# Sixteen row maxima and their scores over ten slots instead of eight, the negation and its transposition after them

## The chip, the core and the metric

The kernel runs on one core of one Trainium2 chip. Its engines are TensorE (PE; its weight loads are listed as PEld), VectorE (DVE), ScalarE (ACT), GpSimd (POOL) and SyncE (SP, which issues most DMAs). Each works through its own instructions in order and waits for the others by semaphores. The metric is the device time of one execution in microseconds (us); lower is better.

## What is computed

One transformer layer on x of shape (4, 2048, 512) in float32. After a layer norm, xn feeds two branches whose results are added to x: attention with keys and values compressed 4 to 1, followed by a Fourier transform, and a feed-forward part with a shared expert and 64 routed experts. The change touches the attention only. Its part of the reference, cut:

```python
qkv = x @ Wqkv
q, k, v = jnp.split(qkv, 3, axis=-1)
k = _compress(k, conv_w, conv_b)          # 2048 positions -> 512
v = _compress(v, conv_w, conv_b)
k = jnp.concatenate([null_k, k], axis=1)  # one key and value more
v = jnp.concatenate([null_v, v], axis=1)
dots = jnp.einsum('bhid,bhjd->bhij', q, k) * d ** (-0.5)
mask = q_idx[:, None] < k_idx[None, :]
dots = jnp.where(mask[None, None], mask_value, dots)
attn = jax.nn.softmax(dots, axis=-1)      # subtracts each row's maximum
out = jnp.einsum('bhij,bhjd->bhid', attn, v)
```

and beside it, in the same stage, the shared expert `jax.nn.silu(xf @ sh_gate_w) * (xf @ sh_up_w) @ sh_down_w` on all 8192 tokens.

## The kernel before

The program runs stage A (layer norm, projections, routing), stage B (`stage_b`, lines 610 to 1443: attention, shared expert, the routed tokens' table), stage E (routed experts) and stage C (output projection and transform). The stages follow one another; the change lies in stage B alone.

**Units.** Attention is cut into 64 units (`NU`): 16 items, one for each batch element and group of four heads, by 4 chunks of 512 queries (`NCH`, `QC`). The chunk's place in its item is n = u % 4. Chunk n needs n + 1 blocks of 128 keys, so its work grows with n.

**Why there are maxima.** A unit's scores are computed twice. First with queries on the partitions: `scores(u, i)` (L1292) for i = 0 to 15, that is four tiles of 128 queries by four heads, writes one bank of `ps_s`; `row_max(u, i)` (L1058) on VectorE reduces it to a column of `mx`. The width is 32 * (4 * n + i // 4 + 1) columns, so it grows with i and with n, up to 512. Then `negate(u)` (L1072) writes -max, split in two parts, into `nm`; `turn_max(u)` (L1316) transposes `nm` on TensorE with four transposes into a `ps_s` bank; and `max_rows(u)` (L961) on ScalarE copies eight rows of it into `q`, as additional rows. With them the second pass, `scores_t(u, kt, h)` (L1323), keys on the partitions, gives scores less their row's maximum, which `exponent` (L967) turns into weights. `scores_null` and `null_exponent` do the same for the additional key.

**The banks.** There are two banks of `ps_s`, used in turn by the sixteen scores and the transposition (`ring_before` L757, `s_bank` L766): 17 uses in a unit. A score waits until the maximum before the last has been read; number 0 waits for the last but one use, number 1 for `max_rows` of the unit before.

**The order.** The order of work is written out by hand, for each engine on its own: a loop over the units, in it a loop over 12 slots k (`SLOTS`), in which each engine takes what is listed for k. In unit u the engines work on the second pass of unit u and on the first pass of unit u + 1. TensorE's slot (L1418 to L1443) begins with six matmuls of 512 columns of the shared expert (`gate_up` in even units and in slots 0 to 3 of odd ones, `down` else). Then come two scores of the next unit (k < 8), up to two `scores_t` (slots 0 to 9 at most), `values` (attention times values, packed matmuls; own chunk in slot 6, others in 7, 9, 11), `denominators` and, in slot 10, `turn_max(u + 1)` and `scores_null(u)`. The first `scores_t` of a unit waits for `mt_emptied`, that is for `max_rows`.

VectorE's slot (L1233 to L1284) holds `up_out`, `gate_out`, `down_out` and `split_h` of the shared expert, `normalise` (slot 1) and `invert` (slots 2 to 5) of the unit before, two `row_max` of the next unit (k < 8), `negate` in slot 8, `add_past` (slots 6, 8, 10 for n = 1, 2, 3 of them) and one step of `group` (L1134), which builds the table of the routed tokens: 16 groups of 36 steps, three units each, so from unit 1 to unit 48. GpSimd masks the diagonal block, multiplies the result (`finish`) and from unit 4 to 51 scatters the table's pairs by indirect DMAs (`scatter`, L931).

TensorE needs from VectorE, in its slots, `gate_out` before slots 4, 8 and the next 0 (semaphore `g_emptied`), `up_out` two slots after it, `down_out(0)` before slot 8 in odd units (`y_emptied`), and the maxima as told above. SyncE loads q two units ahead (`load_q`, L786), once the null scores of the unit before are computed.

Of the kernel before, what the change touches and what calls it, by code (L numbers as in the profile page):

```python
# [599 lines left out]
NU = ITEMS * NCH  # L600
# [9 lines left out]
def stage_b(nc, t):  # L610
    ctx = ExitStack()
    with ctx:
# [153 lines left out]
        def s_bank(u, i):  # L766
            return ps_s[(17 * u + i) % 2]

        def steps(u):

            return u // 2, u % 2 == 0
# [4 lines left out]
        def chunk(part, i):  # L776

            i %= 6
            if i < HJ:
                return part[0][:, i, :, :, :].rearrange("p a k n -> p (a k n)")  # L780
            i -= HJ
            return part[1][:, 2 * i:2 * i + 2, :].rearrange("p j c -> p (j c)")
# [167 lines left out]
        @block.scalar  # L950
        def _(act):
            def split_w(i):
                act.wait_ge(raw_in[i % 2], 32 * (i // 2 + 1))
                j = i % 6
                if i >= 6 and j < HJ:
                    act.wait_ge(u_filled, HJ * (NSTEP - 1) + j + 1)
                elif i >= 6:
                    act.wait_ge(y_filled, TPB * NSTEP)
                act.copy(chunk((wgu_hi, wd_hi), i), raw[i % 2][:, :]).then_inc(w_hi_ready, 1)

            def max_rows(u):  # L961

                act.wait_ge(mt_filled, u + 1)
                act.copy(q[u % 3][3 * DH:KM, :, :], s_bank(u, 16)[3 * DH:KM, None, :].broadcast_to([2 * HPC, HPC, QC]))\
                    .then_inc(mt_emptied, 1)

            def exponent(u, kt, h):  # L967
                i, n = t_index(u, kt, h), u % NCH
                act.wait_ge(t_filled, i + 1)
                if kt == n:  # L970
                    dst = p_diag
                    if u and h == 0:
                        act.wait_ge(pv_done, pv_index(u - 1, (u - 1) % NCH) + 1)
                        if (u - 1) % NCH:
                            act.wait_ge(dve_summed, past_index(u - 1, 0) + 1)
                        else:
                            act.wait_ge(d_filled, u)
                else:
                    c = past_index(u, kt)
                    dst = p_past[c % 2]  # L980
                    if c >= 2 and h == 0:
                        act.wait_ge(pv_done, pv_of_past[c - 2] + 1)
                        act.wait_ge(dve_summed, c - 1)
                act.activation(dst[:, h, :], ps_t[i % 2][:, :], ACT.Exp, scale=SCALE).then_inc(t_emptied, 1)

            pv_of_past = [pv_index(u, kt) for u in range(NU) for kt in range(u % NCH)]

            def null_exponent(u):
                i = t_null(u)
                act.wait_ge(t_filled, i + 1)  # L990
                if u:
                    act.wait_ge(od_emptied, u)
                act.activation(p_null[:, :], ps_t[i % 2][:, :], ACT.Exp, scale=SCALE).then_inc(t_emptied, 1)

            def half_tanh(s, j):
                n = s * HJ + j
                act.wait_ge(g_filled, n + 1)
                if n:
                    act.wait_ge(h_ready, n)
                act.activation(gated[:, :], ps_f[0][:, :], ACT.Tanh, scale=0.5).then_inc(tanh_ready, 1)  # L1000

            def split_h(s, j):
                act.wait_ge(h_ready, s * HJ + j + 1)
                if s:
                    act.wait_ge(y_filled, TPB * s)
                act.copy(hT_hi[:, j, :], hT[:, :]).then_inc(h_hi_ready, 1)

            split_w(0)
            max_rows(0)
            for u in range(NU):  # L1010
                s, gate = steps(u)
                n = u % NCH
                for k in range(SLOTS):
                    if gate and k % 4 == 2:
                        half_tanh(s, k // 4)
                    if gate and k in (5, 9):
                        split_h(s, k // 4 - 1)
                        if s == NSTEP - 1:
                            split_w(6 + k // 4 - 1)
                    if not gate and k == 1:  # L1020
                        split_h(s, 2)
                        if s == NSTEP - 1:
                            split_w(6 + 2)
                    if not gate and k == 2:
                        half_tanh(s, 3)
                    if not gate and k == 4:
                        split_h(s, 3)
                        if s == NSTEP - 1:
                            split_w(6 + 3)
                    if gate and s == NSTEP and k in (3, 4):  # L1030
                        split_w(10 + k - 3)
                    for kt, h in t_slots(n, k):
                        exponent(u, kt, h)
                    if u == 0 and k in (1, 3, 7, 9, 10):
                        split_w((1, 3, 7, 9, 10).index(k) + 1)
                    if k == 11:
                        if u + 1 < NU:
                            max_rows(u + 1)
                        null_exponent(u)

        @block.vector
        def _(dve):
# [189 lines left out]

            for u in range(NU):  # L1233
                s, gate = steps(u)
                for k in range(SLOTS):
                    if gate:
                        if k == 0 and s:
                            down_out(s - 1, 3)
                        if k in (4, 8):
                            up_out(s, k // 4 - 1)  # L1240
                        if k in (6, 10):
                            split_h(s, (k - 6) // 4)
                            if s == NSTEP - 1:
                                split_w(6 + (k - 6) // 4)
                        if k % 4 == 3:
                            gate_out(s, k // 4)
                        if s == NSTEP and k in (5, 7):
                            split_w(10 + (k - 5) // 2)
                    else:
                        if k == 0:  # L1250
                            up_out(s, 2)
                        if k == 2:
                            split_h(s, 2)
                            if s == NSTEP - 1:
                                split_w(8)
                        if k == 3:
                            gate_out(s, 3)
                        if k == 4:
                            up_out(s, 3)
                        if k == 5:  # L1260
                            split_h(s, 3)
                            if s == NSTEP - 1:
                                split_w(9)
                        if k in (7, 8, 10):
                            down_out(s, k // 2 - 3 if k > 7 else 0)
                    if k == 1 and u:
                        normalise(u - 1)
                    if 2 <= k < QTC + 2 and u:
                        invert(u - 1, k - 2)
                    if u + 1 < NU:  # L1270
                        if k < 8:
                            row_max(u + 1, 2 * k)
                            row_max(u + 1, 2 * k + 1)
                        if k == 8:
                            negate(u + 1)
                    if u == 0 and k in (1, 3, 7, 9, 10):
                        split_w((1, 3, 7, 9, 10).index(k) + 1)
                    if k == 9 and u % NCH == 0 and 2 <= u // NCH + 1 < ITEMS:
                        place_null(u // NCH + 1)
                    if k in (6, 8, 10) and (k - 6) // 2 < u % NCH:  # L1280
                        add_past(u, (k - 6) // 2)
                    g, part = (u - 1) // GU_UNITS, (u - 1) % GU_UNITS
                    if 0 <= g < NG:
                        group(g, part * SLOTS + k)  # L1284
# [6 lines left out]
        def _(pe):  # L1291
# [126 lines left out]
            for u in range(NU):  # L1418
                s, gate = steps(u)
                n = u % NCH  # L1420
                for k in range(SLOTS):
# [3 lines left out]
                        gate_up(s, HJ - 1, k // 2, k % 2)  # L1425
                    else:
                        down(s, *DOWNS[k - 4])
                    if u + 1 < NU and k < 8:
                        scores(u + 1, 2 * k)
                        scores(u + 1, 2 * k + 1)  # L1430
                    for kt, h in t_slots(n, k):
                        scores_t(u, kt, h)
                    for kt in pv_slots(n, k):
# [3 lines left out]
                    if k == 0 and u and (u - 1) % NCH:  # L1437
                        denominators(u - 1)
                    if k == 10:
                        if u + 1 < NU:  # L1440
                            turn_max(u + 1)
                        scores_null(u)
            denominators(NU - 1)  # L1443


# [855 lines left out]
```

## Time and profile before

| | us |
|---|---|
| median of 3 runs | 5639.76 |
| lowest and highest | 5633.38, 5650.49 |
| the profiled execution | 5632.38 |
| its span | 5630.6 |

In the profile the table of stretches gives for a stretch of the span the busy time and the number of instructions of each engine, the granted share of TensorE's clock and the DMA engines' share. A wait is idle time of an engine, put down to the instruction whose semaphore ended it; "issue" is time for which nothing is shown, "remote" a signal whose sender isn't shown. The recorded start of a matmul is when it is taken up, its end is modelled. A `DVE_READ_ACCUMULATOR2_ANT` row is the second half of a `row_max` and overlaps what follows, so start to start counts for VectorE.

### The profile page before, as it was taken

The page shows a single profiled execution, that of the slowest core. Times are in us where ns is not written, and L with a number is a line of the kernel's source. Part 1 is how long each engine was busy: PE and PEld are TensorE (multiplying, and loading weights), DVE is VectorE, ACT ScalarE, POOL GpSimd, SP SyncE. Part 2 cuts the span into 40 slices and gives each one's busy share as a digit, 9 for nine tenths or more (in the row PEclk, how much of TensorE's full clock was granted, in tenths as well). Part 3 has the DMA queues.
Part 4 walks back from the last instruction along what each step waited for, and adds up shares of the span by engine and source line. Part 5 has one row for each costly group of instructions (what it writes and reads, how often), then busy time and mean ns, then how long its engine had stood idle before and what let it go on. Part 6 is the DMA issues. An engine that isn't in the chain of part 4 may idle for free. (4 is left out here: it accounts for less than half of the span.)

```text
span 5630.6 us, 101187 instructions
## 1 busy us (share of the span) xinstructions
PE 5462.3 (97%) x33072; PEld 4555.4 (81%) x33072; DVE 3849.7 (68%) x7136; ACT 2578.8 (46%) x3737; POOL 2996.2 (53%) x2620
## 2 busy tenths in 40 slices
PE   8999979999999999999899999999999999999999
PEld 7888866666666666776899999999999999999886
DVE  5444438887778877776666666666666666666656
ACT  3222223333333333333566666666666666666510
POOL 2222202555555555411677777777777777777514
PEclk9999989999999999999999999999999999999999
DMA  6555454434444344432667667677788667676648
GB/s 222 179 179 179 172 161 121 120 110 135 117 129 128 111 130 122 128 113 90 142 116 155 127 130 178 133 156 156 166 206 195 134 118 171 134 155 112 153 173 286
DMA packets 478101, 836.09 MB, mean 148 GB/s; under 512 B 54273, under 2 KB 159490, under 8 KB 475251
## 3 DMA queue, kind: packets, MB, share of 16 engines
q1 hardware_dynamic: 337011, 541.90, 30.3%
q0 software_dynamic: 140928, 292.13, 28.9%
q8 instruction: 90, 1.47, 0.1%
q14 instruction: 72, 0.59, 0.0%
HBM read 501.55 MB, written 332.30 MB: 148 GB/s over the span
## 5 line engine op out<-in xcount | busy, mean ns | idle before, releaser
L1649 POOL DMA_INDIRECT mid_base<-e_rows,e_ox x556 | 1179.0, 2120 | 371.1 <-POOL e_ox L1644 255.7
L1758 DVE TENSOR_TENSOR e_wgu_lo<-e_wgu,e_wgu_hi 128x2048 fp32r<-128x2048 f32 x278 | 637.3, 2292 | 812.5 <-ACT e_wgu_hi L1681 728.8
L1637 POOL DMA_INDIRECT e_xg<-mid_xn,e_ix x556 | 623.2, 1121 | 338.8 <-POOL e_ix L1634 228.0
L1694 ACT CAST e_xT_hi<-e_ps_t 128x512 fp32r<-128x512 f32 x556 | 298.9, 590 | 951.8 <-PE e_ps_t L1824 951.8
L935 POOL DMA_INDIRECT mid_ids<-b_pairs,b_cell x512 | 608.7, 1189 | 148.9 <-issue 147.5
L1837 PE MATMUL e_ps_g<-e_xT_hi,e_wgu_hi 128*128 128x256 f32 x2224 | 652.6, 293 | 1.7 <-DVE e_gated L1775 1.7
L1837 PE MATMUL e_ps_g<-e_xT_lo,e_wgu_hi 128*128 128x256 f32 x2224 | 629.6, 283 | 0.0
L1837 PE MATMUL e_ps_g<-e_xT_hi,e_wgu_lo 128*128 128x256 f32 x2224 | 629.5, 283 | 0.0
L1837 PE MATMUL e_ps_u<-e_xT_hi,e_wgu_lo 128*128 128x256 f32 x2224 | 629.4, 283 | 0.0
L1837 PE MATMUL e_ps_u<-e_xT_hi,e_wgu_hi 128*128 128x256 f32 x2224 | 629.4, 283 | 0.0
L1837 PE MATMUL e_ps_u<-e_xT_lo,e_wgu_hi 128*128 128x256 f32 x2224 | 629.4, 283 | 0.0
L1681 ACT CAST e_wgu_hi<-e_wgu 128x2048 fp32r<-128x2048 f32 x278 | 531.6, 1912 | 28.8 <-DMA e_wgu<-in_up_w 28.8
L1069 DVE CUSTOM_DVE_ANT_0 b_ps_s<-b_ps_s,b_mask 128x34 f32<-128x34 f32 (+14 forms) x960 | 387.3, 440 | 138.3 <-PE b_ps_s L1311 109.1
L1849 PE MATMUL e_ps_y<-e_wd_hi,e_hT_hi 128*128 128x512 f32 x1112 | 436.2, 392 | 0.0
L1849 PE MATMUL e_ps_y<-e_wd_lo,e_hT_hi 128*128 128x512 f32 x1112 | 436.0, 392 | 0.0
L1849 PE MATMUL e_ps_y<-e_wd_hi,e_hT_lo 128*128 128x512 f32 x1112 | 433.6, 390 | 0.0
L1387 PE MATMUL b_ps_f<-b_xT_hi,b_wgu_hi 128*128 128x512 f32 x1024 | 423.0, 413 | 8.5 <-DVE b_gated L1113 8.4
L1837 PEld LDWEIGHTS e_ps_g<-e_xT_hi,e_wgu_hi 128*128 128x128 f32 x2224 | 426.2, 192 | 2.1 <-issue 2.1
L1837 PEld LDWEIGHTS e_ps_g<-e_xT_lo,e_wgu_hi 128*128 128x128 f32 x2224 | 427.6, 192 | 0.0
L1837 PEld LDWEIGHTS e_ps_u<-e_xT_hi,e_wgu_hi 128*128 128x128 f32 x2224 | 427.0, 192 | 0.0
L1837 PEld LDWEIGHTS e_ps_u<-e_xT_lo,e_wgu_hi 128*128 128x128 f32 x2224 | 427.0, 192 | 0.0
L1837 PEld LDWEIGHTS e_ps_u<-e_xT_hi,e_wgu_lo 128*128 128x128 f32 x2224 | 427.0, 192 | 0.0
(257 smaller groups left out, 13413.2 us busy)
## 6 DMA issues: line engine op xcount, KB each, us to landing
b_q<-mid_q_hi SPq DMA_DIRECT2D x128, 256.0 KB
b_xT_hi<-mid_xT_hi SPq DMA_DIRECT2D x32, 1024.0 KB
b_xT_lo<-mid_xT_lo SPq DMA_DIRECT2D x32, 1024.0 KB
mid_base<-b_x SPq DMA_DIRECT2D x32, 1024.0 KB, 7.0
e_wgu<-in_gate_w SPq DMA_DIRECT2D x62, 512.0 KB
e_wgu<-in_up_w SPq DMA_DIRECT2D x62, 512.0 KB
e_wd<-in_down_w SPq DMA_DIRECT2D x62, 512.0 KB
ec_cell<-mid_base SPq DMA_DIRECT2D x88, 256.0 KB, 5.1
```

Of the source, the lines that this page charges most:

```text
L935: pool.indirect_dma_start(t["ids"], bass.IndirectOffsetOnAxis(ap=cell[r][:, i:i + 1], axis=0), pairs[r][:, i, :], None).then_inc(scattered ...
L1069: dve.tensor_tensor_reduce(S[:, 0:n], S[:, 0:n], mask[:, 2 + NC - n:2 + NC], 1.0, floor, ALU.add, ALU.max, mx[:, qt, h:h + 1]).then_inc(s_ ...
L1387: last = pe.matmul(dst[:, :], wt[:, j, a, k, :], xt[:, k, :], start=k == 0 and n == 0, stop=k == DC - 1 and n == 2)
L1637: pool.indirect_dma_start(xg[s][:, i, :], None, t["xn"], bass.IndirectOffsetOnAxis(ap=ix[s][:, i:i + 1], axis=0))\
L1649: pool.indirect_dma_start(t[f"base{i}"], bass.IndirectOffsetOnAxis(ap=ox[s][:, i:i + 1], axis=0), rows[s][:, i, :], None, compute_op=ALU.a ...
L1681: act.copy(wgu_hi[s][:, :], wgu[s][:, :]).then_inc(gu_hi_ready, 1)
L1694: act.copy(xT_hi[s][:, i * DC // 2 * RB:(i + 1) * DC // 2 * RB], ps_t[i][:, :]).then_inc(xT_hi_ready, 1)
L1758: dve.tensor_tensor(wgu_lo[s][:, :], wgu[s][:, :], wgu_hi[s][:, :].bitcast(F32), ALU.subtract)\
L1837: last = pe.matmul(dst[s][:, h * RB:(h + 1) * RB], w[s][:, w0:w0 + P], x[s][:, x0:x0 + RB], start=k == 0 and n == 0, stop=k == DC - 1 and ...
L1849: last = pe.matmul(ps_y[i][:, :], x[s][:, h0:h0 + P], w[s][:, h * DIM:(h + 1) * DIM], start=h == 0 and n == 0, stop=h == HC - 1 and n == 2)
```

## The change

Stage B, three engines. The sixteen scores and maxima of the next unit are no longer taken two per slot in slots 0 to 7, but by `maxima(k)`: 1, 2, 1, 2, 2, 1, 2, 1, 2, 2 in slots 0 to 9 (numbers 0 | 1, 2 | 3 | 4, 5 | 6, 7 | 8 | 9, 10 | 11 | 12, 13 | 14, 15). `negate` moves from slot 8 to slot 10 on VectorE. On TensorE `turn_max` moves from slot 10, ahead of `scores_null`, to the end of slot 11. On ScalarE `null_exponent` comes ahead of `max_rows` in slot 11. No instruction and no semaphore is added.

```diff
+        def maxima(k):
+            return range(16 * k // 10, 16 * (k + 1) // 10) if k < 10 else range(0)
...
                     if k == 11:
+                        null_exponent(u)
                         if u + 1 < NU:
                             max_rows(u + 1)
-                        null_exponent(u)
...
                     if u + 1 < NU:
-                        if k < 8:
-                            row_max(u + 1, 2 * k)
-                            row_max(u + 1, 2 * k + 1)
-                        if k == 8:
+                        for i in maxima(k):
+                            row_max(u + 1, i)
+                        if k == 10:
                             negate(u + 1)
...
-                    if u + 1 < NU and k < 8:
-                        scores(u + 1, 2 * k)
-                        scores(u + 1, 2 * k + 1)
+                    if u + 1 < NU:
+                        for i in maxima(k):
+                            scores(u + 1, i)
...
                     if k == 10:
-                        if u + 1 < NU:
-                            turn_max(u + 1)
                         scores_null(u)
+                    if k == 11 and u + 1 < NU:
+                        turn_max(u + 1)
```

## Rows read from the trace of the kernel before

**Rows 1.** Table of stretches: length, then busy us and instructions of each engine, clock, DMA

```profile
core 0: us, PE busy (x) PEld busy (x) DVE busy (x) ACT busy (x) POOL busy (x), PEclk, DMA share, GB/s
820.00:2340.00 1520.00, 1471.04 (x7003) 995.61 (x7002) 1212.29 (x3206) 536.73 (x838) 801.99 (x769) 1.00 0.43 123
2340.00:2632.00 292.00, 291.38 (x1438) 207.68 (x1438) 218.49 (x552) 106.47 (x168) 39.85 (x53) 1.00 0.40 119
```

**Rows 2.** The same: units 20 to 23, of them 21, 22; units 56 to 59, of them 57, 58

```profile
1391.80:1509.38 117.58, 113.80 (x541) 76.65 (x540) 94.74 (x252) 40.78 (x64) 64.96 (x64) 1.00 0.42 119
1418.53:1449.18 30.65, 27.67 (x121) 18.64 (x120) 24.69 (x62) 8.44 (x13) 16.04 (x17) 1.00 0.35 104
1449.18:1481.14 31.96, 31.49 (x145) 20.24 (x144) 25.35 (x65) 11.80 (x19) 17.86 (x18) 1.00 0.36 108
2440.28:2549.57 109.29, 109.08 (x541) 77.27 (x540) 80.57 (x205) 40.66 (x64) 14.90 (x20) 1.00 0.43 126
2466.19:2491.66 25.47, 25.26 (x121) 18.86 (x120) 19.70 (x50) 8.43 (x13) 3.96 (x5) 1.00 0.40 123
2491.66:2521.27 29.61, 29.61 (x145) 20.72 (x144) 24.38 (x54) 11.80 (x19) 3.65 (x5) 1.00 0.36 108
```

**Rows 3.** Waits of weight loads (sum, times, longest): units 20, 21, 22, then 56 to 59

```profile
PEld b_ps_s L1311 <- DVE b_mx L1069: 1.1, 3, 0.7
...
PEld b_ps_s L1311 <- DVE b_mx L1069: 2.0, 5, 0.9
...
PEld b_ps_f L1409 <- DVE b_x L1132: 1.4, 1, 1.4
...
PEld b_ps_s L1309 <- DVE b_mx L1069: 1.3, 4, 0.4
PEld b_ps_s L1311 <- DVE b_mx L1069: 1.2, 3, 0.4
...
PEld b_ps_s L1311 <- DVE b_mx L1069: 0.9, 4, 0.3
```

**Rows 4.** Timeline of unit 21 (n = 1): start, us, engine, what [idle before <- releaser]

```profile
1425.27 0.47 DVE L1069 CUSTOM_DVE_ANT_0 b_ps_s<-b_ps_s,b_mask 128x290 f32<-128x290 f32 x1 [2.15 <-remote]
...
1440.70 0.55 DVE L1069 CUSTOM_DVE_ANT_0 b_ps_s<-b_ps_s,b_mask 128x386 f32<-128x386 f32 x1
...
1441.18 0.59 DVE L1069 CUSTOM_DVE_ANT_0 b_ps_s<-b_ps_s,b_mask 128x386 f32<-128x386 f32 x1
...
1444.97 0.19 PEld L1409 LDWEIGHTS b_ps_f<-b_wd_hi,b_hT_hi 128*128 128x128 f32 x1 [1.35 <-DVE b_x L1132]
```

**Rows 5.** Timeline of unit 22 (n = 2)

```profile
1456.42 0.60 DVE L1069 CUSTOM_DVE_ANT_0 b_ps_s<-b_ps_s,b_mask 128x418 f32<-128x418 f32 x1 [3.56 <-remote]
...
1471.11 0.76 DVE L1069 CUSTOM_DVE_ANT_0 b_ps_s<-b_ps_s,b_mask,b_s_last 128x512 f32<-128x512 f32 x1
...
1471.78 0.76 DVE L1069 CUSTOM_DVE_ANT_0 b_ps_s<-b_ps_s,b_mask,b_s_last 128x512 f32<-128x512 f32 x1
...
1472.45 2.29 DVE L1091 TENSOR_TENSOR b_p_sum<-b_p_diag,b_p_past 128x2048 f32<-128x2048 f32 x1
...
1474.74 0.68 DVE L1113 SCALAR_TENSOR_TENSOR b_gated<-b_gated,b_ps_f 128x512 f32<-128x512 f32 x1
...
1475.69 0.19 PEld L1387 LDWEIGHTS b_ps_f<-b_xT_hi,b_wgu_hi 128*128 128x128 f32 x1 [0.84 <-DVE b_gated L1113]
```

**Rows 6.** Timeline from the transposition of unit 57's maxima to the first `scores_t`

```profile
2466.19 0.60 PE L1320 MATMUL b_ps_s<-b_ident,b_nm 128*104 128x128 f32 x4
2466.52 0.77 PEld L1336 LDWEIGHTS b_ps_t<-b_q,b_null_lhs 104*128 104x128 f32 x4
...
2466.82 1.86 ACT L964 CAST b_q<-b_ps_s 8x2048 fp32r<-8x2048 f32 x1 [1.20 <-PE b_ps_s L1320]
2467.33 0.19 PEld L1387 LDWEIGHTS b_ps_f<-b_xT_hi,b_wgu_hi 128*128 128x128 f32 x1
...
2468.72 0.19 PEld L1387 LDWEIGHTS b_ps_f<-b_xT_hi,b_wgu_hi 128*128 128x128 f32 x1
...
2470.44 0.33 PEld L1329 LDWEIGHTS b_ps_t<-b_q,b_kc 104*128 104x128 f32 x2
```

## The prediction

> **What bounds the kernel now.** First the table of stretches, cut to the attention stage [rows 1]. It has two regimes. From 820 to 2340 us, while `group` runs on VectorE and `scatter` on GpSimd, TensorE's matmuls are busy 1471.0 of 1520 us (96.8%) and VectorE 1212.3 (80%); from 2340 to 2632 us, without them, matmuls are busy 291.4 of 292. TensorE's clock is granted in full (1.00) in both, so the clock is no term.
>
> Then rounds of four units and single units, cut at the start of `turn_max` [rows 2]; n is the unit's place in its item. A round takes 117.6 us with the groups and 109.3 without. n = 1 takes 30.65 against 25.47, n = 2 takes 31.96 against 29.61; what is left, n = 0 and n = 3 together, 54.97 against 54.21. So n = 1 pays 5.2 us for the groups, n = 2 2.4 and the other two 0.8. There are 12 such rounds, and some 15 units outside them.
>
> The waits of the weight loads [rows 3] say what is paid for: `row_max` is named for 1.1 us in n = 0, for 2.0 in n = 1 and for 2.5 in n = 2 (L1309 and L1311 together). TensorE has scores to compute, and both banks of `ps_s` hold scores that VectorE hasn't reduced.
>
> How far VectorE's order reaches, the timelines tell. In n = 1 [rows 4] VectorE starts its first maximum at 1425.27; slot 8 of TensorE, at 1444.97, has waited for `down_out(0)`, VectorE's first instruction of slot 7. This chain sets slot 8. In n = 2 [rows 5] it starts at 1456.42; `gate_out`, at 1474.74 and some 0.6 long, ends 0.3 us before TensorE's slot 8, at 1475.69, wants it.
>
> **The change, part by part.** No instruction is added or removed.
>
> (1) Maxima later. When VectorE comes to slot 7 it has done 11 maxima instead of 14; numbers 11, 12 and 13 now come behind. In n = 1 maxima of that width start 0.48 us apart, at 1440.70 and 1441.18 [rows 4]: three are 1.5 us, and since the unit loses 5.2, all of it shortens the chain to slot 8: -1.5. In n = 2 they start 0.67 apart, at 1471.11 and 1471.78 [rows 5]: -2.0. In n = 0 the loss named is 1.1 us, and two or three maxima of about 0.4 (estimated between nothing and the 0.48 of the wider ones) stand ahead of it: -1.0. In n = 3 the maxima are those of the next item's first and narrowest chunk and no loss is to be had: 0. Bounds for a round: 0, if VectorE only waits elsewhere, and all that the groups cost, 8.3.
>
> (2) The negation two slots later, its transposition one slot later. Behind `turn_max` ScalarE copies the result in `max_rows`, and the first `scores_t` of the next unit's slot 0 waits for this copy. TensorE is in order: all of its slot 0 and what follows is queued behind. Today slot 10's null scores and all of slot 11 lie between. From an undisturbed unit [rows 6]: the transposes start at 2466.19; the copy starts at 2466.82 (+0.63) and takes 1.86, so it ends at +2.49. TensorE turns to its next weights at 2466.52 (+0.33); six matmuls of `gate_up` take 2468.72 - 2467.33 = 1.39; from the end of the next six (2468.72 + 1.39 = 2470.11) to `scores_t` at 2470.44 are 0.33 for two scores, 0.17 for one. In the new order just these lie between, and `scores_t` comes up at 0.33 + 1.39 + 0.17 = +1.89. TensorE stands from +1.89 to +2.49, 0.6 us, at 63 unit boundaries: 38 us where nothing covers it. Today the cover is 2470.44 - 2466.19 = 4.25 us, more than enough.
>
> Where is it covered afterwards? Where TensorE would only come earlier to a wait for VectorE, in the first slots of n = 1 and n = 2 with the groups. There the first maximum starts 2.15 and 3.56 us after VectorE was ready [rows 4, 5], and VectorE's chain starts from this late signal, not from where TensorE has got to. In n = 1 I take the stall at 0. In n = 2 `normalise` also waits for the denominators, which TensorE computes behind the stalled scores, so the 2.0 above becomes 1.4. In n = 0, in n = 3 and outside the groups it costs its 0.6. Bounds: 0 everywhere, if VectorE leads the whole way, and rival B's price.
>
> (3) The tail. VectorE now has four maxima more between slot 7 and the negation. In n = 2, from the end of `gate_out`: five maxima (3.4), `add_past` 2.3, the operations at L1121 and L1125 and the negation (1.5 together, estimated from the 0.6 of `gate_out`), group operations of 0.1 to 0.4 in each slot: 7.5 to 8.4. TensorE from there to `turn_max`: 0.3 of lead, four slots of 1.39, four scores 0.7, 1.0 for the packed `values` of slot 9, 1.0 for the null scores (estimates from the busy sums of one unit less its six-matmul slots): 8.6. So the negation is in time by 0.2 to 1.1 us. `gate_out(2)` stands behind it (0.6 and a group operation) and TensorE's slot 0 wants it right after the four transposes (0.33): up to 0.7 late. I charge 0.5, and n = 2 is -0.9. n = 1 has one `add_past` less behind slot 7 and over 1 us to spare. Bounds: 0 and 1.5 us in each n = 2 and n = 1.
>
> (4) `null_exponent` ahead of `max_rows` on ScalarE: it takes 0.6 us at a time when the null scores are a whole slot old, and ends before the transposes. `load_q` on SyncE waits for the null scores, which come 0.3 us earlier; nothing waits for it within this unit. Zero; should the null scores be late, `max_rows` behind it is late by as much.
>
> **The sum.** A round with groups: n = 0 -1.0 + 0.6 = -0.4; n = 1 -1.5; n = 2 -0.9; n = 3 +0.6. Together -2.2 us, 12 times -26. Outside the groups 15 stalls, +9, less the waits on VectorE that can go there: the last row of [rows 3] names 0.9 us for maxima in four units, -3; net +6. In all -20 us. The profiled execution took 5632.4 us, its span is 5630.6 and 1.8 lie around it; the median of the runs is 5639.8, 0.13% more. 5632.4 - 20 = 5612, and against the median 5620.
>
> **A rule weighed.** Matmul busy time leaves 49 us idle in the first regime [rows 1]. The Trainium skill (Perfetto Trace Analysis, Identifying the Most-Contended Engine) says that this share is no good measure, and that the busy share of the weight loads is: 995.6 of 1520 is 65.5%, against 71.1% in the second regime, so 8%, 120 us, could be had. By the first reading my gross relief of 12 x 4 us would be all there is; by the second it is under half. The units' lengths, 12 x 8.3 = 100 us, side with the second.
>
> **Rivals.** (A) The forecast as summed: 5602 to 5634, chance 0.45.
>
> (B) TensorE's signal is late for the transposition as well; slower. At the start of n = 1 and n = 2 with groups a score reaches VectorE over 2 us late [rows 4, 5]; what holds it the rows don't say. Today no engine hangs on one quick signal there; after the change `max_rows` does. If it comes 2.6 us late (between the two rows' 2.15 and 3.56), TensorE stands 3.2 us at 24 boundaries, 77 us, and 0.6 at the other 39, 23 us. Against the relief of 12 x 3.9 + 3 = 50 that is +50 with no cover; with half of the 77 covered +11. So 5650 to 5690, 5667 as its middle. It decides once the uncovered part passes (50 - 23) / 24 = 1.1 us per boundary. For it: the row of 3.56 us. Against it: VectorE starts late there anyway. Chance 0.22. The Trainium skill (SBUF — State Buffer, Who interferes with whom) says that TensorE and ScalarE never wait on anyone at the SBUF's ports, and that DMA doesn't contend with a compute engine; by that rule the scatters and loads don't hold the signal, and B has no price. The two rows stay unexplained by it.
>
> (C) The relief is eaten; no change. VectorE has as much to do as before, and the maxima moved to slots 8 and 9 come back as waits for the negation and for `gate_out`. With tails of 1.5 us in n = 1 and n = 2, in place of my 0.5, a round gives 0.3 us: 5640, between 5626 and 5655. Chance 0.25.
>
> (D) More than the forecast: with a shorter queue on VectorE the rest of what the groups cost in n = 1, 5.2 less 1.5, goes nearly whole, `down_out`'s 1.4 us among it [rows 3], and a round gives 3 us more than summed: 5584, 5565 to 5602. Chance 0.08. That the change does nothing at all is no case: the order is written out by hand on three engines.
>
> **Numbers.** A measurement tells 0.3%, 17 us, from no change. Of A 0.31 lies beyond it and 0.14 within; D is 0.08 faster; of C 0.04 is faster, 0.17 within, 0.04 slower; of B 0.18 slower, 0.04 within. Faster 0.43, same 0.35, slower 0.22. The likeliest time is 5620; the range reaches from inside D to the middle of B, 5591 to 5668.
>
> **What would show it.** In slot 0 of n = 3 and n = 0, and in every unit outside the groups, `scores_t` should wait 0.6 us for the copy of L964. The weight loads' waits on `b_mx` should fall by half over 820 to 2340. With groups n = 1 should take 29.1 us, n = 2 31.1, n = 3 0.6 more than before and n = 0 0.4 less; without them a round should grow by about 1 us. A wait for that copy of over 1.5 us at the start of n = 1 or n = 2 is B; waits on `b_gated` or `b_nm` at slots 11 and 0 are C. What would make it wrong above all is the cover in n = 1 and n = 2: it is argued from one late signal each.

## Result, and the profile after

The changed kernel is slower: 5727.1 us median of 4 runs (5722.1 to 5741.9) against 5639.4 (4 runs of the kernel before), ratio 1.0158 (1.0133 to 1.0182), +88 us. The forecast was 5620, in a range from 5591 to 5668.

Each later set of runs was on a chip of its own, and every run is compared with the kernel before in the same set. In the first runs and in three sets *before* takes 5635 to 5640 us; I call these chips *loud*. In three other sets it takes 5598 to 5607; I call them *quiet*. As no two of these sets share a chip, it isn't known whether the difference belongs to the chip or to the time of the set.

The table of stretches, columns as in [rows 1]: units 20 to 23, then each of them, then units 56 to 59 (cut at the last transpose of `turn_max`, which now stands at a unit's end, so compare whole rounds, and n = 1 and n = 2).

```profile
1432.70:1558.03 125.33, 113.40 (x544) 79.30 (x542) 94.70 (x251) 40.76 (x64) 63.70 (x62) 0.96 0.39 112
1432.70:1458.50 25.80, 24.93 (x127) 17.64 (x125) 19.56 (x61) 6.96 (x10) 12.43 (x15) 1.00 0.55 148
1458.50:1494.00 35.50, 27.66 (x123) 20.48 (x122) 24.23 (x61) 9.03 (x14) 16.28 (x16) 0.90 0.31 91
1494.00:1527.80 33.80, 31.21 (x146) 21.08 (x145) 26.69 (x67) 11.78 (x19) 18.01 (x17) 0.95 0.34 101
1527.80:1558.03 30.23, 29.59 (x156) 20.10 (x154) 24.22 (x65) 12.99 (x21) 16.98 (x15) 1.00 0.40 118
2534.50:2645.90 111.40, 109.02 (x542) 77.31 (x541) 81.67 (x204) 40.77 (x64) 14.90 (x20) 1.00 0.42 123
```

The round with groups has grown from 117.6 to 125.3 us [rows 2]. Of these 7.75 us 4.85 lie in n = 1 (35.5 after 30.65) and 1.84 in n = 2 (33.8 after 31.96); n = 0 and n = 3 together took 1.06 more. Outside the groups the round grew from 109.3 to 111.4. The clock, in full before, is granted 0.90 in unit 21.

Waits of the weight loads in unit 21, and from unit 22 the second row of its list:

```profile
PEld b_ps_t L1331 <- issue: 6.5, 1, 6.5
PEld b_ps_f L1411 <- DVE b_x L1135: 1.7, 1, 1.7
PEld b_ps_f L1411 <- DVE b_hT_lo L1128: 1.2, 1, 1.2
...
PEld b_ps_t L1331 <- issue: 2.9, 1, 2.9
```

L1331 is the first `scores_t`. Where [rows 3] showed 2.0 and 2.5 us of waits for maxima, there is one stand of 6.5 and one of 2.9. What it waits for shows in the timeline of unit 21, from the null scores on:

```profile
1455.84 1.10 PE L1338 MATMUL b_ps_t<-b_q,b_null_lhs 104*128 104x512 f32 x4
...
1458.16 0.60 PE L1322 MATMUL b_ps_s<-b_ident,b_nm 128*104 128x128 f32 x4
...
1460.00 0.30 PE L1313 MATMUL b_ps_s<-b_kc,b_q 96*128 96x290 f32 x1
1460.91 0.96 POOL L938 DMA_INDIRECT mid_ids<-b_pairs,b_cell  x1 [0.30 <-issue]
1463.82 0.81 SPq L796 DMA_DIRECT2D b_q<-mid_q_hi  x2
1463.82 0.60 ACT L996 ACTIVATE b_p_null<-b_ps_t 128x512 f32<-128x512 f32 x1 [8.82 <-remote]
1463.90 0.69 DVE L1124 SCALAR_TENSOR_TENSOR b_hT<-b_gated,b_ps_f 128x512 f32<-128x512 f32 x1 [5.07 <-remote]
1464.44 1.86 ACT L967 CAST b_q<-b_ps_s 8x2048 fp32r<-8x2048 f32 x1
1464.51 0.46 DVE L1072 CUSTOM_DVE_ANT_0 b_ps_s<-b_ps_s,b_mask 128x290 f32<-128x290 f32 x1
...
1466.45 1.19 PE L1331 MATMUL b_ps_t<-b_q,b_kc 104*128 104x512 f32 x2 [6.14 <-ACT b_q L967]
...
1467.44 0.63 PE L1389 MATMUL b_ps_f<-b_xT_hi,b_wgu_hi 128*128 128x512 f32 x1
```

The null scores end at 1456.94, and nobody hears of it for 6.9 us. At 1463.82 ScalarE and SyncE start what waits for them, and at 1463.90 VectorE starts `up_out`, which waited for other matmuls: three engines, three signals of TensorE, freed together, while TensorE had gone on to a score at 1460.00. So the signals are late, not the work. `max_rows` (L967) comes behind `null_exponent`, and TensorE stands 6.14 us for it. Then its clock is on the lower level, 1.2 GHz (granted 0.50): a matmul of 512 columns takes 0.63 us instead of 0.39. It is back to the full clock after 1471 us.

```profile
1466.50:1468.00 1.50, 1.50 (x4) 1.21 (x5) 0.06 (x1) 0.75 (x2) 0.08 (x1) 0.50 1.03 220
```

GpSimd's last scatter of a row of eleven starts at 1460.91.

### The profile page after: what moved, and what is told of

The parts are those of the page before. It is cut to its first block and busy times, and to the rows that moved or that the text cites. A ratio compares the mean times of both kernels' runs of the same rounds, so it can differ in the third digit from the quotient of the medians.

```text
span 5726.2 us, 101187 instructions
## 1 busy us (share of the span) xinstructions
PE 5460.5 (95%) x33072; PEld 4582.6 (80%) x33072; DVE 3860.5 (67%) x7136; ACT 2580.8 (45%) x3737; POOL 2995.1 (52%) x2620
## 5 line engine op out<-in xcount | busy, mean ns | idle before, releaser
L931 POOL TENSOR_SCALAR_AFFINE_SELECT b_p_diag<-b_p_diag 128x512 f32<-128x512 f32 x256 | 161.8, 655 | 551.6 <-ACT b_p_diag L987 547.7
L1389 PE MATMUL b_ps_f<-b_xT_hi,b_wgu_hi 128*128 128x512 f32 x1024 | 434.5, 424 | 11.0 <-DVE b_gated L1116 9.9
```

The costliest lines, as they stand in the source:

```text
L931: pool.affine_select(p_diag[:, h, :], p_diag[:, h, :], [[1, QC]], ALU.is_ge, 0.0, base=1 - CF, channel_multiplier=-CF).then_inc(masked, 1)
L1389: last = pe.matmul(dst[:, :], wt[:, j, a, k, :], xt[:, k, :], start=k == 0 and n == 0, stop=k == DC - 1 and n == 2)
```

## Experiments

**The halves.** `turn_late` is *before* with the transposition alone moved (order on ScalarE too):

```diff
                     if k == 10:
-                        if u + 1 < NU:
-                            turn_max(u + 1)
                         scores_null(u)
+                    if k == 11 and u + 1 < NU:
+                        turn_max(u + 1)
```

> The kernel before with one half of the change: turn_max behind scores_null in slot 11 (max_rows behind null_exponent on ScalarE), the maxima still in pairs over slots 0 to 7 and the negation at 8. Theory (TensorE's signals come late at the boundaries into n=1 and n=2 while GpSimd scatters, and the late transposition has nothing left to cover that): it carries more than the whole loss, 5.5 us in n=1, 2.5 in n=2, 0.6 in n=3 and n=0 of each of the 12 rounds and 0.6 at the other 15 boundaries, +100 to +125 us, so 5740 to 5765. Rival (the loss is made by the maxima standing in slots 8 and 9, the transposition costs its 0.6 us a boundary): 63 x 0.6 = +38 us, 5677.

`maxima_spread` is the other half, with the negation at the end of slot 9 (`if k == 9: negate(u + 1)`):

> The other half: the maxima and their scores over slots 0 to 9, the negation at the end of slot 9, turn_max ahead of scores_null in slot 10 as before. Theory: the relief is real and alone here, -20 to -35 us, 5605 to 5620, and the copy of the maxima is in time at nearly every boundary. Rival: 5690, since the waits on the maxima in slots 8 to 10 make the loss.

Two kernels leave out the scatters and their waits, so the routed tokens' table stays blank:

```diff
                     for i in range(part * 4 * TOPK // GU_UNITS, (part + 1) * 4 * TOPK // GU_UNITS):
-                        scatter(g, i)
```

> The changed kernel without GpSimd's scatters of the token table (so the token table stays blank; the groups' work on VectorE stays). Theory: without scatters no signal of TensorE is late, and each boundary costs its 0.6 us: 25 to 40 us over the kernel before without scatters. Rival (the q load or the groups on VectorE hold the signals): +80 to +95 over that kernel, as with scatters, and the waits of 6 us at scores_t stay.

> The kernel before without the scatters. Theory: the late signals of the maxima at the start of n=1 and n=2 go, some 3 to 5 us a round, so 5580 to 5605, and the waits on b_mx of 2.8 and 2.7 us a unit in n=1 and n=2 fall to those of the units behind the groups. Rival: the scatters hold nothing and it stays at 5640 within 10.

On a quiet chip (before 5606.9): `turn_late` 1.0057 (1.0040 to 1.0074), `maxima_spread` 1.0006 (0.9996 to 1.0015), `after_no_scatter` 1.0035 (1.0020 to 1.0049), `before_no_scatter` 0.9986 (0.9977 to 0.9996). The first comes to its rival's figure, the stall alone (+30); the second shows no gain, against both. The kernels without scatters are 31 us apart (5629.2 and 5598.3), as the theory had it, but this doesn't show what the scatters do: no signal was late on this chip with them either, and `before_no_scatter` is in its range of 5580 to 5605 only because *before* takes 5607 here. `maxima_spread` isn't a clean half: its transposition, in slot 10, comes right behind the moved negation, and over the twelve rounds from unit 5 to unit 53 the weight loads wait for `b_nm` 36 times, 30.0 us in all. As the halves don't add up to 88 us, the same kernels were run again elsewhere.

> The changed kernel once more, on a chip of its own choosing: in the last call the kernel before took 5607 us where it had taken 5639, neither half of the change gave more than 0.6%, and no trace of that call shows a late signal of TensorE. Theory (the late signals belong to the chip of the first runs, not to the kernel): if the kernel before takes 5607 again, this one takes 30 to 40 us more, 5635 to 5650, the waits at scores_t are 0.6 us in every unit; if before takes 5639, it takes 5727. Rival (they need both halves together): 5690 or more on any chip, with scores_t waiting 5 to 6 us at the start of n=1.

> The kernel before, for its trace on the chip of this call. Theory: where it takes 5607, row_max follows its score within 0.1 us at the start of n=1 and n=2 too; on the chip of the first trace it followed 2.3 to 2.8 us late. Rival: the delays of 2.3 us are there as well and 5607 comes from another stage.

A loud chip: 5730.7 against 5639.6, ratio 1.0161 (1.0144 to 1.0178); `before_again`, a single run, took 5636.6, and its first `row_max` follows its score 1.6 and 1.3 us late in units 21 and 22. The ratio is the theory's for this kind of chip; the two delays of `before_again` are of the same kind as the first trace's, but smaller than the 2.3 to 2.8 us named there.

> The changed kernel a third time, beside both halves, to have all of them on one chip. So far there were two kinds of chips: before 5639 us with late signals at the start of n=1 and n=2, and before 5607 us (both halves ran there). Theory: where before takes 5639, this takes 5725 to 5735; where it takes 5607, 5635 to 5650, the 0.6 us at each of 63 boundaries and no late signal. Rival (the late signals come from both halves together on any chip): +1.5% there as well.

> The late transposition alone, a second time. Theory: where before takes 5639, TensorE's signals are late and nothing covers them, +1.6 to +2.2%, 5730 to 5760; where before takes 5607, +0.5 to +0.6% as measured. Rival (it needs the maxima in slots 8 and 9 and the negation at 10 as well): +0.6% on either chip.

> The spread maxima alone, a second time. Theory: where before takes 5639 it is a gain of 10 to 30 us, since the transposition in slot 10 covers the late signals and the maxima leave DVE room; where before takes 5607, 0 as measured. Rival: the late signals now meet score matmuls in slots 8 and 9, +20 us or more.

> The changed kernel without GpSimd's scatters, a second time. Theory (the late signals need the scatters): +0.3 to +0.4% over before on a chip where before takes 5607 (as measured), -0.4 to 0% where it takes 5639, with 0.6 us at scores_t in every unit. Rival (something else than the scatters holds them, and the first chip had none): +1.5% where before takes 5639.

Loud again (before 5634.9): the changed kernel 1.0161 (1.0144 to 1.0178), `turn_late` 1.0073 (1.0056 to 1.0090), where 1.6 to 2.2% was expected, `maxima_spread` 1.0064 (1.0048 to 1.0081), its rival's figure, and without scatters 0.9974 (0.9962 to 0.9985). So the late signals need the scatters, and both halves together cost 95 us, more than 39 and 39. What the late signals take of this shows when the twelve rounds are compared on a loud and on a quiet chip: `turn_late` takes 1425.9 and 1386.8 us, 39 more on the loud one, `maxima_spread` 1428.7 and 1367.6, 61 more, and *before* loses 47 (below). So the late transposition alone loses no more to them than *before* does, the spread maxima alone 14 us more, and the two together 61 more. `maxima_spread` has run on both kinds of chip with eleven scatters around the same `max_rows`. Timelines, GpSimd's first and last scatter and then ScalarE, first quiet, then loud:

```profile
1399.55 1.00 POOL L938 DMA_INDIRECT mid_ids<-b_pairs,b_cell  x1 [0.16 <-issue]
...
1412.28 1.02 POOL L938 DMA_INDIRECT mid_ids<-b_pairs,b_cell  x1 [0.30 <-issue]
...
1407.89 1.87 ACT L967 CAST b_q<-b_ps_s 8x2048 fp32r<-8x2048 f32 x1 [1.56 <-PE b_ps_s L1322]
```

```profile
1429.30 1.00 POOL L938 DMA_INDIRECT mid_ids<-b_pairs,b_cell  x1 [0.16 <-issue]
...
1442.49 0.96 POOL L938 DMA_INDIRECT mid_ids<-b_pairs,b_cell  x1 [0.30 <-issue]
...
1442.83 1.86 ACT L967 CAST b_q<-b_ps_s 8x2048 fp32r<-8x2048 f32 x1 [6.72 <-remote]
```

The transposes start 7.7 us after the first scatter on the quiet chip and 8.5 us on the loud one. The copy starts 8.3 us after it on the quiet chip and 13.5 us on the loud one, where the signal is put down to no one ("remote"), as in unit 21 above.

**How long the row of scatters is.** GpSimd issues ten or eleven scatters in every unit. I count as a row those that start one every 1.26 us up to the copy; a scatter that itself takes longer (1.3 to 2.9 us) ends a row. In the first trace of the changed kernel the copy starts 5.1 to 5.7 us late at the seven boundaries with eleven in the row, 3.7 to 4.0 at the four with nine, 1.6 to 2.3 at the eleven with eight, 1.0 at two with six and seven, and never at the starts of n = 3 and n = 0, where the row has one to four. The count isn't a sharp rule: in `turn_late_2` five copies are 0.9 us late behind four, and in `after_again` one is 5.0 us late though the seventh of its eleven scatters takes 1.49 us and leaves four behind it. Three kernels test the length. `after_split` and `before_split` issue the first five scatters of a unit (`first` to `end`) ahead of `finish`, where GpSimd is idle:

```diff
                 mask_diagonal(u)
+                if 0 <= g < NG:
+                    for i in range(first, first + 5):
+                        scatter(g, i)
                 if u:
                     finish(u - 1)
...
                 if 0 <= g < NG:
-                    for i in range(part * 4 * TOPK // GU_UNITS, (part + 1) * 4 * TOPK // GU_UNITS):
+                    for i in range(first + 5, end):
                         scatter(g, i)
```

> The changed kernel with its scatters in two runs: five of the ten or eleven of a unit ahead of finish, where GpSimd is idle for 6 to 8 us, the rest behind it. Nothing else is moved. Theory (TensorE's signals are held back while GpSimd is in an unbroken run of more than some five to eight scatters, and only on some chips): no run is longer than six and none reaches the end of the unit, so no signal is late on any chip: 5615 to 5630 where before takes 5639, 5630 to 5640 where it takes 5607. Rival 1 (each scatter holds the signals for its own time): the late signals move to the middle of the unit and the time stays at 5700 or more. Rival 2 (the late signals come from the transfers, not from GpSimd): they stay at the start of n=1 and n=2.

> The kernel before with the same two runs of scatters. Theory: 5595 to 5610 on any chip, that is some 30 us under before where that takes 5639 and level with it where it takes 5607. Rival: no change on either chip.

`after_gap` leaves them behind `finish`, and before the fifth adds `pool.wait_ge(s_emptied, 16 * (u + 1) + 15)`, the maximum of slot 9:

> The changed kernel with one wait in the run: GpSimd issues four scatters behind finish, then waits for the row maximum ahead of the last one, then issues the rest, which now run further into the next unit. Theory (it is the length of the unbroken run): two runs of four and six, the signals in time or late by at most 1 us where before takes 5639, 5620 to 5650. Rival (what counts is that scatters run over the boundary): as late as in the changed kernel or later, 5725 or more.

> The kernel before without scatters, for the chip of this call. Theory: 5595 to 5605 on any chip, that is -0.6% where before takes 5639 and -0.15% where it takes 5607. Rival (the scatters cost before nothing, its late maxima have another cause): 5630 where before takes 5639.

A loud chip (before 5636.6): `after_split` 5619.8, 0.9974 (0.9964 to 0.9984); `before_split` 5592.7, **0.9929** (0.9912 to 0.9946), 44 us faster than before; `after_gap` 5651.2, 1.0029 (1.0018 to 1.0041); `before_no_scatter` 5584.9, 0.9917 (0.9901 to 0.9934). Stretches of twelve rounds with scatters (from the transposition of unit 5 to that of unit 53): before, the changed kernel, `before_split`, `before_no_scatter`, `after_split`, `after_gap`, all loud.

```profile
950.00:2357.30 1407.30, 1362.89 (x6482) 920.91 (x6481) 1121.99 (x2968) 494.73 (x774) 782.50 (x747) 1.00 0.43 122
```

```profile
960.30:2448.30 1488.00, 1356.83 (x6484) 948.27 (x6482) 1126.18 (x2968) 495.31 (x775) 775.07 (x745) 0.97 0.40 116
```

```profile
953.10:2313.60 1360.50, 1334.04 (x6482) 923.77 (x6481) 1126.82 (x2968) 494.43 (x774) 768.36 (x742) 1.00 0.44 126
```

```profile
948.40:2308.90 1360.50, 1334.20 (x6482) 923.78 (x6481) 1123.40 (x2968) 494.25 (x774) 184.91 (x240) 1.00 0.43 126
```

```profile
960.40:2340.80 1380.40, 1324.82 (x6483) 924.19 (x6481) 1132.11 (x2968) 494.71 (x774) 738.09 (x742) 1.00 0.43 125
```

```profile
959.70:2371.50 1411.80, 1342.44 (x6483) 921.84 (x6481) 1138.18 (x2968) 492.13 (x774) 764.13 (x746) 1.00 0.42 122
```

With the scatters in two rows the stretch is as long as with no scatters at all, 1360.5 us: late signals had cost *before* 47 us there. The changed kernel loses 108 us to them (1488.0 less 1380.4). `before_no_scatter` is 8 us below `before_split` all the same, and below the 5595 that was expected at least; these 8 us lie outside the stretch, and nothing here tells their cause. In `after_gap` GpSimd's timeline shows the break of 2.31 us and behind it seven scatters in a row:

```profile
1424.13 0.96 POOL L938 DMA_INDIRECT mid_ids<-b_pairs,b_cell  x1 [0.30 <-issue]
1427.40 0.96 POOL L938 DMA_INDIRECT mid_ids<-b_pairs,b_cell  x1 [2.31 <-DVE b_mx L1075]
...
1435.13 0.95 POOL L938 DMA_INDIRECT mid_ids<-b_pairs,b_cell  x1 [0.30 <-issue]
```

They run across the end of the unit at 1430.6, and no copy of the maxima is late anywhere. But other signals are. In unit 19 (n = 3) a row of seven, from 1371.33 on, ends so:

```profile
1378.91 0.96 POOL L938 DMA_INDIRECT mid_ids<-b_pairs,b_cell  x1 [0.31 <-issue]
1378.92 0.29 PE L1316 MATMUL b_ps_s<-b_kc,b_q 96*128 96x34 f32 x2
...
1381.29 0.20 DVE L1075 CUSTOM_DVE_ANT_0 b_ps_s<-b_ps_s,b_mask 128x34 f32<-128x34 f32 x1 [2.17 <-remote]
1381.35 1.09 ACT L990 ACTIVATE b_p_diag<-b_ps_t 128x512 f32<-128x512 f32 x2 [3.48 <-remote]
```

The scores are done at 1379.21 and the `scores_t` behind them at 1379.8, and VectorE and ScalarE start on them together at 1381.3. Between 950 and 2340 us their waits for TensorE name "remote" nine times, 24.0 us in all, and in `after_split` never. So scatters over the boundary aren't what delays the copy, and breaking the row shrinks the delays but doesn't remove them: seven in a row held signals in unit 19 and not in the row above. The time, 5651, is 1 us over what the theory allowed. The stretch is 31 us longer than in `after_split`; the weight loads wait 41.9 us for `b_mx` in it, there 9.8, so held scores are part of it. The masks of the diagonal, now queued behind the scatters, may be another part; the two weren't separated. The length isn't all either: in *before* and in `turn_late` on the loud chip signals are late by 0.8 to 2.4 us behind six scatters.

**What of a scatter it is.** In `after_plain` each scatter is a plain transfer, `pool.dma_start(t["idle"][first:first + P, :], pairs[r][:, i, :])`; in `after_busy` it is eight `pool.iota` of two columns.

> The changed kernel with each scatter replaced by a plain transfer of the same 1 KB issued by GpSimd in the same place (to a spare table; the token table stays blank). It tells apart what of a scatter holds TensorE's signals. Theory (GpSimd's issuing of descriptors for any of its own transfers does it): late signals at the start of n=1 and n=2 in so far as the issues still come without a break; with shorter issues, less. Rival (it is the indirect addressing): none, and the time of the changed kernel without scatters, -0.3% where before takes 5635 to 5640, +0.4% where it takes 5607.

> The changed kernel with each scatter replaced by eight tiny iota instructions on GpSimd, no transfer (the token table stays blank). Theory (the transfers' issuing holds the signals, not that GpSimd is at work): no late signal, -0.3% where before takes 5635 to 5640. Rival (any work of GpSimd without a break does it): late as in the changed kernel, if the eight take about as long as a scatter, 1.2 us.

> The spread maxima alone (transposition in slot 10) with the scatters in two runs, to be read against the kernel before with the scatters in two runs, 5593 us where before took 5637 (ratio 0.993). The forecast gave the spread maxima -26 us. Theory (that relief was read from waits which the late signals had made, so it is worth nothing without them): 5593 to 5605 where before takes 5637, ratio 0.993 to 0.996. Rival (the relief is real): 5565 to 5575, ratio 0.987 to 0.989.

These ran on a quiet chip (before 5597.9), where nothing is late with scatters either, so the first two can't settle it. `after_busy` took 1.0035 (1.0021 to 1.0049), as without scatters; its instructions also kept GpSimd busy for less, 485 us over twelve rounds, where the scatters made it 775 in the first trace. `after_plain` took 1.0310 (1.0293 to 1.0327) for another reason; its weight loads in units 20 to 23:

```profile
PEld b_ps_f L1389 <- DMA b_xT_lo<-mid_xT_lo: 9.7, 2, 6.3
```

The shared expert's inputs land late, a wait that no other kernel has. `spread_split` took 1.0009 (1.0000 to 1.0019): no gain from spread maxima. Its partner `before_split` wasn't run here; over the twelve rounds `spread_split` takes 1365.2 us, 5 more than the 1360.5 of `before_split`.

> The changed kernel once more; it has only run where the kernel before takes 5635 to 5640 us, three times, at +1.6%. On the two chips where before takes 5598 to 5607 both halves and the kernels without scatters ran with no late signal. Theory: on such a chip this takes +0.4 to +0.6%, 5620 to 5640, which is the 0.6 us at 63 boundaries and nothing else; on a chip of the first kind +1.6% once more, which says nothing new. Rival: the two halves together make the signals late on any chip, +1.6%.

This was a quiet chip: 5626.7 against 5599.1, ratio 1.0047 (1.0030 to 1.0063). The round of units 20 to 23, unit 21 of it, and the start of unit 21:

```profile
1394.40:1509.10 114.70, 110.17 (x542) 76.96 (x540) 95.19 (x251) 40.77 (x64) 64.19 (x62) 1.00 0.42 122
...
1420.20:1448.70 28.50, 25.98 (x122) 18.65 (x121) 24.40 (x61) 8.43 (x13) 16.66 (x17) 1.00 0.37 113
```

```profile
1419.87 0.60 PE L1322 MATMUL b_ps_s<-b_ident,b_nm 128*104 128x128 f32 x4
...
1420.51 1.86 ACT L967 CAST b_q<-b_ps_s 8x2048 fp32r<-8x2048 f32 x1 [1.22 <-PE b_ps_s L1322]
...
1422.51 0.71 PE L1331 MATMUL b_ps_t<-b_q,b_kc 104*128 104x512 f32 x2 [0.52 <-ACT b_q L967]
```

The copy starts 0.64 us after the first transpose and TensorE stands 0.52 us, as it does in every unit of this trace. Unit 21 takes 28.5 us, 7.0 less than on the loud chip; of these the shorter stand is 6.14 - 0.52 = 5.6, and the clock the rest, about 1.4.

## Why the prediction was wrong

**The stall of 0.6 us (part 2)** is right in place and size. Outside the groups `turn_late` has rounds of 112.10 us where before has 109.29, that is 0.7 at each of four boundaries, and the whole of it costs 5637.0 - 5606.9 = 30 us on a quiet chip; 38 were reckoned for 63 boundaries with nothing covered.

Two steps of the prediction failed: the cover of the stall, and the relief. The fall of 20 us was the sum of a relief of 54 (4.5 a round), stalls of 22 and a tail of 6 in the rounds with groups, and 6 outside. In the same twelve rounds the late signals cost 61 us that no term had, and the relief is worth 5.

**The cover in n = 1 and n = 2** is the step that failed first. The stall was set to 0 in n = 1 and to its bare 0.6 in n = 2, as VectorE would start late anyway. On a quiet chip there is no late start and thus no cover: TensorE stands 0.52 in these units too. On a loud chip the late signal hits the copy itself, and TensorE's stand of 0.6 grows to 6.5 and 2.9 us. That is rival B's mechanism, with its point of decision (1.1 us uncovered) passed. Its price was mis-sized: 3.2 us per boundary from the two rows of 2.15 and 3.56, where the two stands of this round make 9.4 us in place of 6.4, and the clock adds 1.4 each time. I took the delay for a constant of 2.6 us. It isn't one: it varies with the scatters around it. Ahead of unit 21's start *before* issues eleven too, but the fifth takes 1.61 us and six follow it; in the changed kernel none of the eleven takes over 1.00.

**The relief of the maxima (part 1)**, 54 us in all and the term that made the forecast a gain, is nearly absent. Waits on `b_mx` did fall, as forecast: in n = 1 from 2.0 us [rows 3] to nothing in unit 21's list. But compare unit 21 where no signal is late, waits of the weight loads in `before_split` and then in the changed kernel on a quiet chip:

```profile
PEld b_ps_s L1315 <- DVE b_mx L1073: 1.7, 4, 0.8
PEld b_ps_f L1413 <- DVE b_x L1136: 1.4, 1, 1.4
...
PEld b_ps_f L1413 <- DVE b_hT_lo L1129: 0.7, 1, 0.7
```

```profile
PEld b_ps_f L1411 <- DVE b_x L1135: 1.7, 1, 1.7
...
PEld b_ps_f L1411 <- DVE b_hT_lo L1128: 1.2, 1, 1.2
PEld b_ps_t L1331 <- issue: 0.8, 1, 0.8
```

Of the 1.7 us for maxima, 0.3 come back for `down_out` and 0.5 for `split_h`; 0.8 more stand at `scores_t`, the stall of part 2, and unit 21 takes 28.4 and 28.5 us. The waits over all twelve rounds show it with the stall on both sides, in `turn_late` and then in the changed kernel, both on quiet chips:

```profile
PEld b_ps_s L1311 <- DVE b_mx L1069: 27.1, 86, 1.3
PEld b_ps_f L1387 <- DVE b_gated L1113: 16.0, 19, 2.5
...
PEld b_ps_f L1409 <- DVE b_hT_lo L1125: 8.1, 12, 0.8
```

```profile
PEld b_ps_f L1389 <- DVE b_gated L1116: 27.0, 26, 3.0
...
PEld b_ps_f L1411 <- DVE b_hT_lo L1128: 13.1, 12, 1.2
PEld b_ps_s L1313 <- DVE b_mx L1072: 13.0, 32, 1.4
```

With the smaller rows of other lines, `b_mx` falls from 38.4 to 18.4 us, by half as forecast, and `b_gated` gains 11.0 and `b_hT_lo` 5.0. This is rival C's mechanism, VectorE with as much to do as before, and its largest part is the wait for `gate_out` that C named. Over these rounds the changed kernel takes 1381.8 us and `turn_late` 1386.8: relief of 0.4 us a round, where 4.5 were summed (3.9 once the stall in n = 2 is taken off). The other runs fit: `maxima_spread` +3 us and `spread_split` +5 on quiet chips, both with the waits for the negation that their own order makes. My misreading was to price relief by what n = 1 and n = 2 lose to the groups (5.2 and 2.4 us, rows 2). On the loud chip of those rows 3.9 us a round of this, (1407.3 - 1360.5) / 12, was late signals and not VectorE's queue.

**The tail (part 3)** was charged in n = 2 with 0.5. For the negation it wasn't needed: the weight loads wait for `b_nm` once in the twelve rounds, 1.2 us. In unit 22 `b_gated` is waited for 1.0 us, no more than before; that wait grew in other units, as said. C's own sum has a slip: with tails of 1.5 us in both units a round loses 0.3 us and doesn't give it, which makes some 5650 and not 5640, still inside C's bounds. **The order on ScalarE (part 4)** costs nothing by itself, but its clause came true: with the null scores late, `max_rows` was late by as much.

**The bill** of the stretch on the loud chip: without late signals the change costs 1380.4 - 1360.5 = 20 us, and outside it 2.1 us a round, 8 us in all; late signals cost 108 instead of 47, +61. Together +89; +88 was measured.

**The rule weighed beside rival B** (the Trainium skill, SBUF — State Buffer, Who interferes with whom: TensorE waits for no one at the ports, DMA doesn't contend with compute) would give the scatters no price. No run here shows TensorE's matmuls slowed at the ports, but its signals do depend on the scatters: take these away, and 108 us go. The measurement decides. The other rule (the Trainium skill, Perfetto Trace Analysis, Identifying the Most-Contended Engine) put what could be had at 120 us, the idle time of the matmuls at 49. The groups cost *before* 1407.3 - 12 x 109.3 = 96 us in the twelve rounds, nearer to the 120. `before_split` got 47 of it, and the rest is still there: 113.4 us a round against 109.3.

**Open**: why a row of scatters holds TensorE's signals, whether it needs GpSimd's transfers or their indirect addresses, whether the row's length or the moment at which a signal falls into it counts, and whether it depends on the chip or on the time of the set. `before_split` wasn't run on a quiet chip.

## What to carry to other kernels

A wait that is "covered" by another engine's lateness is covered only as long as that lateness has a known cause; when a row says "remote" and a start is microseconds late, find its cause first, for the next instruction hung on the same kind of signal pays it in full. Moving work out of one wait of a busy engine shortens nothing if the same engine is asked for the next thing right after: count what it still has to do up to the later wait. Scatters that GpSimd issues in a long row are better split around its other work: two rows a unit made the kernel before 0.7% faster on a loud chip. On quiet chips only the spread maxima were run both ways, and the twelve rounds took 1367.6 us with one row and 1365.2 with two.

## What the runs showed of the hardware

- Several signals of TensorE were held up to 6.9 us (1456.94 to 1463.82) and then freed together within 0.1 us, while its instructions went on; three other engines stood meanwhile.
- It needed GpSimd's indirect scatters: delays of 1.6 us and more at the copy came mostly behind eight or more, 1.26 us apart, smaller ones behind six or seven too. The four sets of runs on loud chips have it; in the traces of quiet chips it never shows, with rows of nine and eleven, and *before* takes 0.5 to 0.7% less time there.
- After a stand of 6.1 us TensorE's matmuls of 512 columns took 0.63 us in place of 0.39, with the clock granted 0.50; over the twelve rounds it was granted 0.97.
